# A fused token tower (gather, attention, routed FFN): single signals per product on TensorE, and a drain in another order

## The reference, cut to what matters

```python
# 1. tokens: three gathered tables (64, 64 and 24 wide), each through a small product and GELU, fused to 64
item_emb = emb_table[ids]; geo = geo_table[ids]; visit = visit_table[ids]
cat = concat(gelu(item_emb @ w_item + b), gelu(geo @ w_geo + b), gelu(visit @ w_visit + b))
h = item_emb + 0.1 * layer_norm(gelu(cat @ w_fuse + b)) * valid
# 2. attention: 4 heads of 16 over the 128 tokens of a row, softmax, out rounded to bf16, then Wo
h = h + attn(layernorm(h))
# 3. routed FFN on x = layernorm(h): of the 128 tokens of a row the 63 with the highest weight get the FFN
weights = x @ wr + br                               # (128 rows, 128 tokens)
_, idx = top_k(weights, 64); sel_idx = idx[:, :63]  # ties: the lower index first
y = (gelu(x[sel] @ w1 + b1) @ w2 + b2) * weights[sel]
out = h + x + scatter(y to sel_idx)
```

## Time and profile before

| | |
|---|---|
| median of 3 runs | 552.93 us (550.33 to 558.99) |
| the profiled execution's own time | 557.61 us |
| its span, first to last instruction | 555.7 us |
| mean granted clock of TensorE | 0.938 |
| PE, DVE, ACT, POOL busy | 82%, 76%, 68%, 63% |
| bytes written to HBM | 4.19 MB |

### The profile page before, as it was taken

One profiled execution on the slowest core, in us unless ns is written; L12 is line 12 of the kernel. 1 busy time (PEld: TensorE's weight loads), 2 busy tenths in 40 slices (PEclk: granted clock), 3 DMA queues, 4 the chain that ended last, 5 costly groups with the idle time before them and its releaser, 6 DMA issues. The chain is left out here.

```text
span 555.7 us, 16674 instructions
## 1 busy us (share of the span) xinstructions
PE 456.0 (82%) x5850; PEld 346.8 (62%) x5850; DVE 420.0 (76%) x1648; ACT 377.8 (68%) x662; POOL 350.6 (63%) x412
## 2 busy tenths in 40 slices
PE   4778788888898888988988988888988789968670
PEld 2445576676666566766666666666767666756460
DVE  1367788877877888888777777888886658887486
ACT  1236677787877777777877778777776667846550
POOL 5746676676666676666766676667666547541574
PEclk9788999999999999999999999999997889998855
DMA  3211111111111111111111111111111111000046
GB/s 96 31 21 28 27 21 19 26 23 23 23 23 23 23 17 18 18 17 23 23 23 23 23 23 23 23 17 18 18 17 21 23 20 14 13 2 3 21 122 162
DMA packets 23733, 15.72 MB, mean 28 GB/s; under 512 B 18848, under 2 KB 21536, under 8 KB 23712
## 3 DMA queue, kind: packets, MB, share of 16 engines
q0 software_dynamic: 6144, 9.97, 12.1%
q1 hardware_dynamic: 17568, 5.48, 3.7%
HBM read 10.98 MB, written 4.19 MB: 27 GB/s over the span
## 5 line engine op out<-in xcount | busy, mean ns | idle before, releaser
L335 POOL TENSOR_TENSOR rs<-ve,minus_half 128x4 f32<-128x4 f32 x96 | 103.8, 1091 | 68.6 <-DVE ve L677 67.2
L327 POOL DMA_INDIRECT G<-table,idx x64 | 66.2, 1034 | 57.6 <-issue 47.7
L770 DVE TENSOR_REDUCE neg_max<-psum 128x4 f32<-128x512 f32 x128 | 84.4, 680 | 5.4 <-PE psum L1124 5.4
L327 POOL DMA_INDIRECT G<-turned,idx x64 | 60.7, 948 | 19.5 <-issue 19.5
L1052 PE MATMUL psum<-wt,hid 128*128 128x64 f32 x512 | 69.8, 294 | 2.5 <-ACT hid L471 1.5
L464 ACT ACTIVATE prob<-psum 128x512 f32<-128x512 f32 x128 | 66.1, 602 | 5.3 <-PE psum L1094 3.5
L1052 PEld LDWEIGHTS psum<-wt,hid 128*128 128x128 f32 x512 | 66.1, 208 | 3.3 <-ACT hid L471 2.2
L1094 PE MATMUL psum<-q_s,k_s 32*128 32x128 f32 x1024 | 39.1, 288 | 28.6 <-issue 23.5
L1094 PEld LDWEIGHTS psum<-q_s,k_s 32*128 32x128 f32 x1024 | 33.4, 191 | 35.5 <-issue 29.2
L814 DVE TENSOR_SCALAR k_s<-psum,wt 128x512 f32<-128x512 f32 x32 | 24.0, 751 | 31.7 <-PE psum L1211 31.0
L1124 PE MATMUL psum<-k_s,q_s 32*128 32x128 f32 x1024 | 41.1, 301 | 3.5 <-ACT prob L464 3.5
(11 more groups left out here) (116 smaller groups left out, 1108.5 us busy)
## 6 DMA issues: line engine op xcount, KB each, us to landing
out<-R SPq DMA_DIRECT2D x13, 256.0 KB, 2.6
G<-table,idx POOLq DMA_INDIRECT x64
G<-turned,idx POOLq DMA_INDIRECT x64
wt<-packed SPq DMA_DIRECT2D x1, 932.0 KB, 4.8
q_s<-max_t SPq DMA_DIRECT2D x32, 8.0 KB
out<-R SPq DMA_DIRECT2D x1, 512.0 KB, 4.3
out<-R SPq DMA_DIRECT2D x2, 128.0 KB, 3.5
ids_sb<-ids SPq DMA_DIRECT2D x1, 64.0 KB, 1.9
```

The source lines that it names most:

```text
L327: pool.indirect_dma_start(G[par][:, b, :], None, turned if b >= 2 else table, bass.IndirectOffsetOnAxis(ap=idx[par][:, b:b + 1], axis=0),) ...
L335: pool.tensor_tensor(rs[:, :], ve[:, :], minus_half[:, :], ALU.pow).then_inc(S[dst], 1)
L770: dve.tensor_reduce(neg_max[:, GB * h:GB * h + GB], bank[h].rearrange("p (b k) -> p b k", b=GB), AX, ALU.max, negate=True).then_inc(S["max ...
```

## The change: what it does

**Single signals.** On TensorE `scores`, `scores_t` raise one semaphore after the last product instead of four (one per head), `queries` and `keys` one instead of two, `ffn_first` one instead of four: 11 fewer in a step. Those who wait now wait for that one.

**Half the ranking in regular steps.** Parts are rows 0 to 63 and 64 to 119. VectorE and TensorE leave their loops at i = SPLIT = 18; steps 18 to 29 are straight code. The built program of TensorE grows from 199 rows to 455 (a row is one instruction or a run of equal ones), that of VectorE from 387 to 646; the three others change by at most 16 rows. GpSimd, ScalarE and SyncE keep their loops. Step 18 has the transpose and copy of W for rows 0 to 63, steps 19 to 25 one round each (between `divide` and `keys_out`), step 26 `select`, step 27 the transpose back and `take_coef`. In steps 18 and 27 TensorE waits for VectorE's copy before the value product, which uses the same PSUM bank.

**The last two groups by comparison.** For groups 30 and 31 TensorE spreads each weight row over 128 partitions (`wide`), and VectorE counts for each token how many are above it or equal with a lower index (`compare`): 8 operations of 128 x 128, one reduction, one small selection. For group 31 the FFN's product is taken from PSUM straight into R (`shift_routed`, `finish`).

**Order of the drain.** GpSimd adds rows 0 to 63 from step 29 on between its other work, each time with the reciprocal root and the routing product of the next group placed around the sums; ScalarE multiplies pieces 8 to 11 and 14; the rounds of part 1 are spread over VectorE's waits; stores follow in another order, one more than before. Five filler products (`keep_busy`) stand on TensorE near the end.

```diff
+HALF = P // 2
+TAIL = P - 2 * GB
+PARTS = ((0, HALF), (HALF, TAIL))
+SPLIT = 18
+SUMS = tuple((n, 8) for n in range(0, TAIL, 8)) + ((TAIL, GB),)
+ACT_SCALED = (8, 9, 10, 11, 14)
+POOL_SUMMED = (0, 1, 2, 3, 4, 5, 6, 7, 12, 13)
+DVE_SUMMED = (8, 9, 10, 11, 14, 15)
+STORES = POOL_SUMMED[:8] + (8, 9, 12, 10, 11, 13, 14, 15)
...
+            turns = ((NG - ahead if end is None else end) - FIRST) // 2
...
# GpSimd, drain
             rstd(ve3, rs3, "ve3_ready", "rs3_ready", NG - 4)
+            add_routed(1)
             weighted(NG - 4)
             add_x3(NG - 4)
+            add_routed(2)
             rstd(ve3, rs3, "ve3_ready", "rs3_ready", NG - 3)
             weighted(NG - 3)
             add_x3(NG - 3)
-            pool.wait_ge(coef_ready, 1)
-            wait(pool, "y_ready", 1, TAIL // GB - 1)
-            add_routed(0)
+            add_routed(3)
+            add_routed(4)
             rstd(ve3, rs3, "ve3_ready", "rs3_ready", NG - 2)
...
# VectorE
+            def compare(g):
+                dve.wait_ge(wide_ready, g - TAIL // GB + 1)
+                for b in range(GB):
+                    wide, own = bank[RANK_BANK[g]][:, b * P:(b + 1) * P], wb[g % 2][:, b:b + 1]
+                    last = dve.scalar_tensor_tensor(equal[:, b, :], wide, own, lower[:, :],
+                                                    ALU.is_equal, ALU.mult)
+                done(last)
+                for b in range(GB):
+                    wide, own = bank[RANK_BANK[g]][:, b * P:(b + 1) * P], wb[g % 2][:, b:b + 1]
+                    last = dve.scalar_tensor_tensor(above[:, b, :], wide, own, equal[:, b, :],
+                                                    ALU.is_gt, ALU.add)
+                done(last)
+                done(dve.tensor_reduce(rank[:, :], above[:, :, :], AX, ALU.add))
+                dve.scalar_tensor_tensor(of(coef, g), rank[:, :], float(KEEP), wb[g % 2][:, :],
+                                         ALU.is_lt, ALU.mult).then_inc(rank_done, 1)
...
+                if type(i) is int and SPLIT < i <= SPLIT + KEEP // 8:
+                    rounds(0, i - SPLIT - 1, i - SPLIT)
+                if type(i) is int and i == SPLIT + KEEP // 8 + 1:
+                    select(0)
...
# VectorE, last part of the drain
             center(c3, of(R, NG - 1), mv3, "c3_ready", NG - 1)
-            wait(dve, "r_ready", 1, TAIL // GB - 1)
-            add_routed(0)
+            select(1)
             norm3(NG - 1)
+            take_coef(1)
             ffn_out(NG - 2)
             route(NG - 1)
-            add_routed(1)
-            take_weights(1)
-            rounds(1, 0, KEEP // 8)
-            select(1)
-            ffn_out(NG - 1)
-            add_routed(2)
-            take_coef(1)
-            add_routed(3)
-            add_routed(4)
-            add_routed(5)
-            add_routed(6)
-            add_routed(7)
+            with_bias(NG - 1)
+            compare(NG - 2)
+            add_routed(8)
+            compare(NG - 1)
+            shift_routed(NG - 1)
+            add_routed(9)
+            finish(NG - 1)
+            add_routed(10)
+            add_routed(11)
+            add_routed(14)
+            add_routed(15)
...
# TensorE
+                if type(i) is int and i == SPLIT:
+                    wait(pe, "qs_ready", 1, b)
+                    weights_t(0)
+                    pe.wait_ge(rank_in, 1)
...
-            pipeline(pe, step)
+            pipeline(pe, step, end=SPLIT)
```

241 lines of the change are left out of this document (145 added, 96 removed).

## The result

The changed kernel takes 569.1 us (median of 4 runs, 565.1 to 572.0) where the kernel before took 555.7 in the same session: ratio 1.0265, 95% interval 1.0201 to 1.0328, slower. Run once more later it gave 1.0207 (1.0142 to 1.0271), 565.0 us. The forecast was 544.7 us; what came is 24 us above it and on the other side. The profiled execution took 569.1 us, its span is 567.3 us.

A forecast was written before the change was run, and what follows sets the result against it. VectorE's chain through a step was taken to bound the kernel. Terms summed to -8.2 us: 549.4 from the profiled 557.6, or 544.7 from the 552.9 median; range by its bounds 540 to 550, for 8 in 10 536.5 to 552.5 us.

The forecast's parts named there:

- Seven rounds in steps 19 to 25: VectorE: each round of 0.70 us fits the 0.78 us hole before k_s: 0; 4.9 us if the hole closes.
- the lateness of o_t: VectorE's loop steps: o_t starts 0.50 us later than in straight code; left in the sum as unchanged.
- the stalls near 421 and 438 us: Between 416.85 and 470.92 us of the profile: 8.7 us over three steps, taken for noise of that execution.
- The copies in steps 18 and 27: TensorE's value product waits for VectorE's copy: 1.2 us each, +2.4 us; bounds 0.35 and 1.47 us each.
- the second rival: Steps 18 and 27: the added waits let TensorE's clock fall, +5.8 to +8.7 us, 550.5 to 553.4 us; chance 0.14.
- Straight code: VectorE leaves its loop 10 steps sooner, saving 0.44 us a step: -4.4 us; bounds -2.9 and -9.1 us.
- That straight code itself stalls: TensorE's 12 newly straight steps stall 2.9 us each on instruction transfers: 580 us; chance 0.06.
- Single signals: 11 fewer signals a step let k_s and o_t come 0.02 us sooner: -0.5 us; bounds 0 and -1.1 us.
- The drain, first half: Up to the end of group 31's `c`, with group 30's root starting with its input: -3.7 us; bounds 0 and -4.7.
- The drain, second half: Behind group 31's `c`: VectorE's list takes 17.1 us, but stores limit the gain to -2.5 us; bounds 0 and -3.5.
- Contention: Drain: GpSimd's sums beside VectorE's work delay one operation on the chain, +0.5 us; bounds 0 and +4 us.
- the reordered steps ahead of it: Step from 485.13 to 501.33 us: W's transpose and copy go, 0.9 us; TensorE's new order costs about as much: 0.

The follow-up runs named there:

- a_one_gather: The changed kernel with one gather of the four of a group, the rest of the tiles constant: 519.0 us, ratio 0.933 to the kernel before.
- a_unranked: The changed kernel without the first half's ranking (coefficients 0 to 63 set to one), straight code kept: 551.7 us, ratio 0.996 to the kernel before.
- b_signals: The kernel before, loops kept, with the change's single signals and their waits alone: 550.9 us, ratio 0.996.
- b_both: The kernel before with single signals and with steps 18 to 27 of TensorE and VectorE as straight code: 550.2 us, ratio 0.990.
- b_straight: The kernel before with steps 18 to 27 of TensorE and VectorE written out as straight code, nothing else changed: 552.8 us, ratio 0.998.
- a_rounds_late: The changed kernel with each round of the first half behind the variances, some 9 us behind k_s: 558.4 us, ratio 1.003 to the kernel before.
- b_setup: The kernel before with the two instructions added that fill `lower` on VectorE ahead of the first step: 553.5 us, ratio 0.999.
- b_both_again: The kernel before with single signals and straight code once more, on the chip where the kernel before takes 526.8 us: 525.4 us, ratio 0.998.
- a_no_y_wait: The changed kernel without the added wait for Y ahead of the transposition of x3: 559.5 us, ratio 1.016 to the kernel before.

## Why the prediction was wrong

**The step that failed is "Seven rounds in steps 19 to 25", costed at 0.** The hole ahead of k_s was there and the round went into it, and in a_one_gather, without the late signals, that cost nothing, as I had it. With the four gathers it cost 4.9 us over six steps in the profile (94.1 against 89.2 us in a_unranked), and together with the copies it came with executions that are all at 563 us or more. I had priced the hole closing, at 4.9 us for seven rounds; that this is the same figure is chance, since 0.23 us of the hole stayed open. What I had taken for fixed is the hole's neighbour, the lateness of o_t: it has levels, and at the higher ones TensorE's clock can fall to half. The rows for it were there: the stalls near 421 and 438 us, which I set aside as noise, are V and o_t seen 2 to 3 us late among gathers, and the first of them comes in nearly every profile with four gathers on those chips. Without the first half's ranking the changed kernel is at 0.996; with it at 1.02 to 1.03. The range was too narrow besides: with all terms at their worse ends my own bounds reach 557 us, and 562 with the rounds' 4.9, not 550.

**The copies in steps 18 and 27** (+2.4): mis-sized, by the second rival. Either the waiting is covered (step 18 at 15.07 us in the first profile), or the clock falls and it is 3 to 5 us. Step 27 stalled in both profiles of the changed kernel (22.5 and 20.7 us), at o_t, ahead of the copy; with rounds only or copies only it took 16.3 and 15.4 us. But b_signals and b_both, which have neither rounds nor copies in their steps, take 20.4 us there in their profiles, with o_t 3.0 us late as well: the stall isn't the ranking's own.

**A term that was missing: the start.** +5 us, by a stretch at half clock, taken back by leaving out one wait that I had given no cost at all.

**Straight code** (-4.4): right in sign, too large. a_unranked's six steps gain 1.5 us on its looped twin's (89.2 for 90.7), 0.25 us a step for my 0.44; b_straight as a whole 1 us. The stretches I compared differ in the lateness behind o_t too, so not all of the 0.44 us was the code's. Nor was the straight step at 470.92 free of gathers, as I wrote: the last one was issued at 472.55. On the chip without lateness only 0.05 us is left. **That straight code itself stalls**, my rival that ended slower, is refuted by b_straight: it had the right sign for a wrong reason.

**Single signals** (-0.5): 0.996, so -2.2 us with 0 to -4.2 as its interval; my bounds, 0 to -1.1, hold only the smaller part of it. The Trainium skill's serialized increments (TensorE: Matmul & The Clock Gate, "The cost: per-tile semaphore tail") would make it -3.7, which the interval holds as well; no run here tells the two apart.

**The drain, first half** (-3.7): right where the clock holds, -3.6 us (26.1 for 29.7) in the second profile, and the root of group 30 starts with its input; in the first profile the clock fell there and it is +1.4 us, a case that I hadn't priced. **The drain, second half** (-2.5): the list is as long as I had it (17.2 us, forecast 17.1), though partly by luck: `shift_routed` took 2.6 us for my 1.1, the adds 3.3 for 5.0. But the stores end 6.9 us behind the last add instead of 4.2, so 0.6 us is left in that pair of profiles. As a whole, from the last k_s, nine profiles with the old drain take 54.4 to 60.4 us (median 56.2), nine with the new one 50.2 to 50.9: -5.7 us, for my -5.7. The two others, the changed kernel's first profile and a_rounds_late, take 55.2, both with a half clock in it, where next to nothing is left. What I had at 0, the reordered steps ahead of it, gives some 3 us back (from k_s of step 28 to that of step 30 32.2 to 36.3 us, for 29.9 to 31.0 in eight of nine old ones; 32.6 for 29.9 with one gather). **Contention** (+0.5): too small. In `shift_routed` an add of 256 columns took 1.37 us beside GpSimd's sum (551.02 in the second profile, and as long in the first one), for 0.42 alone; that one delay is 1 us.

Summed by what the runs show for the changed kernel, against the kernel before: start +5, signals -2, straight code -1.5, rounds with the lateness beside them +5, steps ahead of the drain +3, drain -6, in all +3.5 us. Measured are 11 to 15 us. The 8 to 11 us between are left for the stalls in steps 18 and 25 to 27. The profiles agree: in either of them the changed kernel takes some 8.5 us more there than b_setup, which is at 0.999 and whose profile has no stall of 3 us. But the kernel before has such stalls too, in some executions: its own profile loses 7.5 us in steps 25 to 27. Between the two first profiles (11.6 us) the stalls therefore cancel but for 1.1 us, and the start makes 4.7, the rounds' steps 3.5, steps 28 and 29 3.0 and the drain 0.9 (steps 3 to 17 give 1.5 back). That the stalls come in more executions with the ranking is what the medians say; no run counts them.

What stays open: what in a gather delays the signals of another engine, why it comes in levels of 0.7 us, why one of the chips is free of it, and on the others step 28 in most profiles (o_t at 0.44 us in the kernel before, with a gather under way), why rounds and copies together cost more than either alone, why the clock falls behind one idle time of TensorE and not behind another as long, and how a wait that never waits brings on the half clock at the start.

## What to carry to other kernels

A hole in an engine's timeline is room for work only if the wait that ends it is of fixed length; look first whether the wait has several levels over the run, and what is in flight when it is long. Stalls that fall on the same place in several profiles are the kernel's, even when they look like noise in one. And where an edit can leave TensorE idle for 2 us more, price the half clock that may follow (4 us or more here) as well as the idle time, and give it a chance: behind 2.2 us without a product it came in one kernel and stayed away in another.

## What the runs showed of the hardware that was not expected

- Among four gathers of 128 rows (0.95 us of GpSimd each), a product of TensorE is seen by VectorE 0.5, 1.2, 1.9 or 2.6 us late, and by ScalarE late too; with one gather per group it isn't (0.44 us from the transposes' start in steps 2 to 29), nor in step 25, where no gather lies beside the transposes. The bytes matter little (64 for 608 a row: 0.992). It costs 1 us of a 15.1-us step, and 7% of the kernel's time (ratio 0.930 with one gather).
- The chips differ in it: the kernel before took 554 to 558 us on four of them and 526.8 us on the fifth, where a kernel with the same gathers (b_both_again) has o_t at 0.44 us in steps 3 to 29.
- Idle times of TensorE of 2.2 and 2.9 us had it at half clock behind them, one of 1.1 us with 0.4 us more behind it as well (a_one_gather, step 18); the steps cost 5 to 7 us more. But 2.20 us in a_no_y_wait left it at 1.00, and in the drain the same 1.22 and 0.83 us had 0.50 behind them in one profile of the changed kernel and 1.00 in the other.
